# A transformer layer on eight cores: first projection started behind a quarter of the input, value projection in half-size groups with two store queues

## What is computed

```python
q, k, v = (proj(wq), proj(wk), proj(wv))          # x @ w.T, split in 16 heads
q, k = apply_rope(q, k, sin, cos)
att = softmax(einsum('bhqd,bhkd->bhqk', q, k) / sqrt(HD))
y = einsum('bhqk,bhkd->bhqd', att, v)             # then y @ wo.T
x = layernorm(x + attention)
x = layernorm(x + ffn(x))                         # gate, up, silu, down; int weights
```

## Time and profile before

| | us |
|---|---|
| median of 3 runs | 4934.71 |
| lowest of them | 4930.45 |
| the profiled execution | 4929.0 |
| its span on the slowest core (core 1) | 4927.5 |
| spans of the eight cores | 4909.2 to 4927.5 |

### The profile page before, as it was taken

The page is one execution under the profiler, slowest core; times in us unless marked ns, Lnnn a source line. Parts: engine busy times, 40 slices in busy tenths (PEclk is TensorE's granted clock), DMA queues, the critical chain, the costliest instruction groups (busy, mean ns, idle before and its releaser), DMA issues.

```text
span 4927.5 us, 42276 instructions; the slowest of 8 cores (4909.2 to 4927.5 us)
## 1 busy us (share of the span) xinstructions
PE 3875.9 (79%) x15680; PEld 1494.9 (30%) x15680; DVE 635.9 (13%) x1592; ACT 1313.9 (27%) x1073; POOL 357.5 (7%) x680
## 2 busy tenths in 40 slices
PE   3999766677777777777967999989921999998870
PEld 1444322211111111112423444433310444443330
DVE  0222000001010000101220000011121000011122
ACT  0111101343434333343442333300022333320003
POOL 0000000000000000000000000012200000002220
PEclk9999888888878787888988999998965999999995
DMA  6334310110100101001574444344435444434443
GB/s 121 58 75 96 70 40 26 29 22 14 26 13 13 26 13 26 13 13 26 167 192 81 75 76 77 71 65 60 61 86 120 77 76 75 75 68 63 63 53 119
DMA packets 200713, 310.96 MB, mean 63 GB/s; under 512 B 99265, under 2 KB 152642, under 8 KB 191682
## 3 DMA queue, kind: packets, MB, share of 16 engines
q0 software_dynamic: 97344, 188.85, 23.9%
q1 hardware_dynamic: 103170, 119.41, 8.1%
HBM read 412.86 MB, written 58.72 MB: 96 GB/s over the span
## 4 chain that ended last, share of the span: by engine, by line
PE 66%; DMA 16%; ACT 5%; DVE 5%; issue 5%; another core or an unknown queue 2%; SPq 0%; DVEq 0%; ACTq 0%; POOLq 0%; POOL 0%
PE PS L585 12%; PE PS L592 12%; PE PS L478 9%; DMA AB<-wd_c 7%; PE PS L530 6%; PE PS L526 5%; PE PS L493 5%; PE PS L563 5%; PE PS L606 4%; PE PS L515 4%; ACT AB L639 3%; PE PS L518 3%; DMA AB<-AB 2%; DMA v_sp<-AB 2%; DMA AB<-x1b 2%
## 5 line engine op out<-in xcount | busy, mean ns | idle before, releaser
L585 PE MATMUL PS<-AB 128*128 128x512 bf16 x2816 | 627.1, 381 | 267.9 <-DMA AB<-x1b 267.9
L639 ACT ACTIVATE AB<-PS,AB 128x1024 bf16<-128x1024 f32 x512 | 563.1, 1113 | 853.0 <-PE PS L518 853.0
L606 PE MATMUL PS<-AB 128*128 128x512 bf16 x2816 | 672.3, 397 | 83.4 <-DVE AB L794 82.1
L592 PE MATMUL PS<-AB 128*128 128x512 bf16 x2816 | 622.1, 379 | 0.0
L478 PE MATMUL PS<-AB 128*128 128x512 bf16 x2048 | 445.1, 381 | 78.1 <-DMA AB<-wq_c 78.1
L515 PE MATMUL PS<-AB 128*128 128x512 bf16 x512 | 247.3, 483 | 299.4 <-DVE AB L744 277.6
L585 PEld LDWEIGHTS PS<-AB 128*128 128x128 bf16 x2816 | 276.8, 98 | 604.1 <-issue 275.3
L526 PE MATMUL PS<-AB 128*128 128x512 bf16 x896 | 393.7, 439 | 37.1 <-ACT AB L639 37.1
L606 PEld LDWEIGHTS PS<-AB 128*128 128x128 bf16 x2816 | 273.7, 101 | 482.0 <-issue 265.8
L530 PE MATMUL PS<-AB 128*1 128x512 bf16 x896 | 377.4, 421 | 0.0
L592 PEld LDWEIGHTS PS<-AB 128*128 128x128 bf16 x2816 | 275.3, 98 | 332.5
(11 more groups left out here) (71 smaller groups left out, 1741.9 us busy)
## 6 DMA issues: line engine op xcount, KB each, us to landing
AB<-wg_c POOLq DMA_DIRECT2D x88, 512.0 KB, 6.1
AB<-wu_c POOLq DMA_DIRECT2D x88, 512.0 KB, 8.1
AB<-wd_c POOLq DMA_DIRECT2D x352, 128.0 KB, 2.9
AB<-x SPq DMA_DIRECT2D x16, 1024.0 KB, 6.6
x1f<-AB SPq DMA_DIRECT2D x16, 1024.0 KB, 4.9
AB<-x1f SPq DMA_DIRECT2D x16, 1024.0 KB, 6.7
out<-AB SPq DMA_DIRECT2D x16, 1024.0 KB, 4.7
AB<-xT POOLq DMA_DIRECT2D x16, 512.0 KB, 33.3
```

The lines of the kernel that those rows point to most:

```text
L585: mm = t.matmul(bank(par * 4 + cch)[:, 0:512], GDQ[par][:, di * 128:(di + 1) * 128], X1T[:, di * 1024 + cch * 512: di * 1024 + (cch + 1) * ...
L592: mm = t.matmul(bank(par * 4 + 2 + cch)[:, 0:512], UDQ[par][:, di * 128:(di + 1) * 128], X1T[:, di * 1024 + cch * 512: di * 1024 + (cch + ...
L606: mm = t.matmul(bank(tt)[:, 0:512], HT[:, h2 * 1024 + tt * 128: h2 * 1024 + (tt + 1) * 128], WDQ[i % 2][:, 0:512], start=(h2 == 0), stop=( ...
L639: sc.activation(PT[u % 4], bank(2 * (u % 2), 2)[:, 0:1024], AF.Exp, bias=CVC[:, 0:1], scale=ASCL).then_inc(s2sc, 1)
```

## The change

It has two parts. At the start, POOL issues only four blocks of the input, then the first two query weights, then the other twelve blocks in three batches of four, each batch after everything of the batches before has landed, and the value weight last. PE waits for a quarter of the input at a time during its first head block. In the value projection there are 16 groups of 64 matmuls that alternate between the two halves of PSUM, so that PE waits only for the copies of the group before the last; the staging buffer has four parts; the even stores stay on SP's queue, and the odd ones are issued by ACT itself on its own queue (semaphore `s1spv`). The rest of the program is as before; two scratch areas move to make room.

```diff
-    VST = [bf16(OFF_VSTG + i * 1024, 128, 512) for i in range(2)]
+    VST = [bf16(OFF_VSTG + i * 1024, 128, 512) for i in range(4)]
...
 sync
-            for i in range(64):
-                jb, tt = divmod(i, 8)
-                dc, th = divmod(jb, 2)
+            for i2 in range(32):
+                i = 2 * i2
+                j2, t2 = divmod(i, 4)
+                dc, q = divmod(j2, 4)
                 s.wait_ge(s1scb, i + 1)
-                if i >= 1:
-                    s.wait_ge(s1spb, 16 * i)
-                s.dma_start(out=v_sp[th * 8 + tt][:, dc * 512:(dc + 1) * 512],
-                            in_=VST[i % 2]).then_inc(s1spb, 16)
+                if i2 >= 1:
+                    s.wait_ge(s1spb, 16 * i2)
+                s.dma_start(out=v_sp[q * 4 + t2][:, dc * 512:(dc + 1) * 512],
+                            in_=VST[i % 4]).then_inc(s1spb, 16)
...
 gpsimd
-            for dt in range(NDI):
+            for dt in range(4):
                 g.dma_start(out=XT[:, dt * 2048:(dt + 1) * 2048],
                             in_=xT_h[dt * 128:(dt + 1) * 128, :]).then_inc(s0x, 16)
+            if PH >= 1:
+                g.dma_start(out=WB[0], in_=wq_h[0]).then_inc(s1w[0], 16)
+                g.dma_start(out=WB[1], in_=wq_h[1]).then_inc(s1w[1], 16)
+            for b in range(1, 4):
+                g.wait_ge(s0x, 16 * 4 * b)
+                for dt in range(4 * b, 4 * b + 4):
+                    g.dma_start(out=XT[:, dt * 2048:(dt + 1) * 2048],
+                                in_=xT_h[dt * 128:(dt + 1) * 128, :]).then_inc(s0x, 16)
...
-                    g.wait_ge(s1pb, 2 * (dc - 1))
+                    g.wait_ge(s1pb, 4 * (dc - 1))
...
 tensor
-            t.wait_ge(s0x, 16 * NDI)
...
                 for di in range(NDI):
+                    if j == 0 and di % 4 == 0:
+                        t.wait_ge(s0x, 16 * min(4 * (di // 4 + 1), NDI))
...
-            for jb in range(8):
-                dc, th = divmod(jb, 2)
-                if th == 0:
+            for j2 in range(16):
+                dc, q = divmod(j2, 4)
+                if q == 0:
                     t.wait_ge(s1vw[dc % 2], 16 * (dc // 2 + 1))
-                if jb >= 1:
-                    t.wait_ge(s1scb, jb * 8)
+                if j2 >= 2:
+                    t.wait_ge(s1scb, 4 * (j2 - 1))
                 for di in range(NDI):
-                    for tt in range(8):
-                        tg = th * 8 + tt
-                        mm = t.matmul(bank(tt)[:, 0:512],
+                    for t2 in range(4):
+                        tg = q * 4 + t2
+                        mm = t.matmul(bank((j2 % 2) * 4 + t2)[:, 0:512],
...
 scalar
+            def vspill(i):
+                j2s, t2s = divmod(i, 4)
+                dcs, qs = divmod(j2s, 4)
+                sc.wait_ge(s1scb, i + 1)
+                if i >= 3:
+                    sc.wait_ge(s1spv, 16 * ((i - 1) // 2))
+                sc.dma_start(out=v_sp[qs * 4 + t2s][:, dcs * 512:(dcs + 1) * 512],
+                             in_=VST[i % 4]).then_inc(s1spv, 16)
+            for j2 in range(16):
+                sc.wait_ge(s1pb, j2 + 1)
+                for t2 in range(4):
+                    i = j2 * 4 + t2
+                    if i >= 4:
+                        sc.wait_ge(s1spb if i % 2 == 0 else s1spv,
+                                   16 * ((i - 4) // 2 + 1))
+                    sc.copy(VST[i % 4], bank((j2 % 2) * 4 + t2)[:, 0:512]).then_inc(s1scb, 1)
+                    if i >= 2 and i % 2 == 0:
+                        vspill(i - 1)
+            vspill(63)
```

More of the change, by code:

```diff
@@ L41 @@
 OFF_SDB   = 203888
-OFF_SPC   = 199168
-OFF_SPC2  = 200192
+OFF_SPC   = 200704
+OFF_SPC2  = 201728
 OFF_XT    = 0
@@ L230, in build_program @@
     s1v1 = sem("s1v1"); s1sw = sem("s1sw"); s1v2 = sem("s1v2"); s1sp = sem("s1sp")
-    s1vw = [sem("s1vwA"), sem("s1vwB")]; s1pb = sem("s1pb"); s1scb = sem("s1scb"); s1spb = sem("s1spb")
+    s1vw = [sem("s1vwA"), sem("s1vwB")]; s1pb = sem("s1pb"); s1scb = sem("s1scb"); s1spb = sem("s1spb"); s1spv = sem("s1spv")
     s2kv = [sem("s2kvA"), sem("s2kvB")]; s2st = sem("s2st"); s2pv = sem("s2pv"); s2sc = sem("s2sc")
@@ L288, in _ @@
                 s.wait_ge(s1sp, 16 * 16)
-                s.wait_ge(s1spb, 16 * 64)
+                s.wait_ge(s1spb, 16 * 32)
+                s.wait_ge(s1spv, 16 * 32)
                 if DEBUG:
@@ L397, in _ @@
             g.dma_start(out=VW[0], in_=wv_h[0]).then_inc(s1vw[0], 16)
-            for j in range(32):
+            for j in range(2, 32):
                 src = wq_h[j] if j < 16 else wk_h[j - 16]
-                if j >= 2:
-                    g.wait_ge(s1pe, j - 1)
-                    g.wait_ge(s1w[j % 2], 16 * (j // 2))
+                g.wait_ge(s1pe, j - 1)
+                g.wait_ge(s1w[j % 2], 16 * (j // 2))
                 g.dma_start(out=WB[j % 2], in_=src).then_inc(s1w[j % 2], 16)
```

## The result

The changed kernel takes 4777.95 us (median of 10 runs) against 4934.79 us for the kernel before (median of 10). Their ratio is 0.9687, with a 95% interval of 0.9675 to 0.9698. The forecast was 4788 us with a range of 4763 to 4814: it held, and the size was right within 10 us of 157. That it came so near is partly luck. One of its terms, the stall at a reload, was wrong by 14.7 us, and another one, the start, by 4 us in the opposite direction.

A forecast was written before the change was run, and what follows sets the result against it. PE's two waits, 78.1 us before the first matmul and 118.5 us in the value projection, were taken to bound the kernel. Gains 15.6 + 127.9 = 143.5 us off 4929.0 gave 4785.5, plus 3: 4788 us, range 4763 to 4814.

The forecast's parts named there:

- Part 1, the start: Start, up to the end of head block 1: it ends at 93.3 us instead of 108.9, gain 15.6 us.
- the dry queue: Start: behind input batches 2 and 3 nothing is queued, costing 2.4 us for each of two batches.
- the lower bound: Start: the last input block lands at 68.0 us if the load queue never runs dry.
- Part 2, PE's work: Value projection: PE's matmuls take 16 x 13.81 = 221.0 us, with all seven 12.4 us gaps gone.
- Part 2, the stalls: Value projection, third and fourth weight reloads: PE stalls 5.35 us at each, 10.7 us, plus 4.0 us for the clock.
- Part 2, the end: End of value projection: three chained stores on ACT, 7.0 us until SP may load k and v, before 15.6.
- Rival 1: Value projection: stores pass the reload over two queues, no stall; gain 158.2 us, time 4774 us; chance 0.20.
- Rival 2: Start gains only 0 to 8.6 us, queue dry longer or block 2's weight late; 4795 to 4804 us; chance 0.12.
- Rival 3: Value projection: granted clock does not hold high without rests; 5009 us worst, 4839 at 13/16 clock; chance 0.04.
- the prediction's sign: PE's matmuls: the forecast is wrong if the granted clock leaves 1.00 while PE is busy; no size given.
- Rival 4: Value projection: ACT's and SP's stores disturb each other, 16.9 us a store; time 5102 us; chance 0.02.
- Rival 5: Value projection: PE still waits for the current group's copies, so the change does not do what it says; chance 0.02.

## Why the prediction was right, and where it was wrong

**What bounds the kernel.** Right. The two waits lay on the chain, and what was taken from them came off the end; the rest of the program is as long as before within a few microseconds.

**Part 1, the start.** Forecast 15.6 us, measured 11.7 on average over the cores. The mis-sized term is the dry queue: 2.4 us for each of two batches. On core 2 PE's bursts start at 42.48, 59.42 and 77.11, so the third batch took 16.9 us and the fourth 17.7, where 13.8 + 2.4 = 16.2 was forecast, and the second ended at 42.4 instead of 40.4. Without the waits the bursts are 12.3 and 12.2 us apart (43.54, 55.80, 67.96 on core 3), the whole comes to the 68.0 of the lower bound, and the two batches cost 8.1 instead of 4.8. The slow matmuls after the idle time cost 1.7 us instead of 3.2, and the copy of block 1 came at 96.15 against 93.3. PE's first matmul was forecast near 25 us; it came at 33.6, although the first four blocks had landed by 21.69, when POOL issued the next ones. The row names the input; by the row of the run without batch waits it was held by small tables that I had not looked at, but that time is hidden by the later quarters. The weight of block 2 was in time, as forecast: PE ran on through 192 matmuls.

**Part 2, PE's work.** 221.0 forecast; measured 222.9 on five cores and 221.2 on the three others. The difference is a short stretch at the low clock just after the 2.3 us wait ahead of the stage, while PE is busy. Core 2:

```profile
513.80:517.00 3.20, 3.20 (x9) 1.10 (x8) 1.19 (x2) 0.00 (x0) 0.00 (x0) 0.50 0.23 52
517.20:735.60 218.40, 218.40 (x1012) 98.82 (x1010) 1.22 (x1) 33.32 (x60) 1.58 (x3) 1.00 0.28 68
```

The prediction had put nothing for it. In the kernel before it came on five cores too, but not on core 1, from which the forecast was made.

**Part 2, the stalls.** This is the step that failed: "Store 11 is issued about 0.7 us after the group's end, behind the reload by 0.2 us". It was issued 0.33 us ahead of it. I had let a DMA issue on ACT wait for the end of the copy that stands before it in the list, where it waits only for its semaphore; and the whole term hung on 0.2 us. With the store held back by one copy, the stall appeared, 5.1 to 10.3 us per core for both reloads instead of the 10.7 forecast, since the reloads landed sooner (13.8 to 17.4 us) than what I took from core 1.

**Part 2, the end.** 7.0 forecast, 743.02 - 735.63 = 7.4 measured on core 2 and 6.9 on average, 1.6 us less than with one queue by the run without the second (8.5).

**The sum.** On core 2 the value projection took 230.3 us against 242.8, so 12.5 too much was forecast here, and 2.9 too little at the start (93.3 against 96.15). The load of k was forecast at 752.7 and came 9.6 us earlier. From there on this core took 3.1 us longer than core 1 before, which leaves 6.5 us in the profiled execution. The rest is the step to the median: I had added 3 us, rounded down by half a microsecond, and the median lies 1.1 us below the profiled execution. So a forecast that had only left out the stall (14.7 us) would have said 4773 and been 5 us low: the errors offset each other in part.

**The rivals.** Rival 1 came nearer to the time (4774) than the forecast did, but not by its mechanism: stores do not pass a reload. In the changed kernel store 13 and SP's store 12, both behind it, took 15.9 and 17.1 us, and the store held back by one copy took 13.6 to 17.5. Here the trace again disagrees with what the page "DMA: Bandwidth & Descriptors" of the Trainium skill says in "Queues, rings and completion order" on turns between queues, now for a second queue as well. Rival 2 was half right in size (4 us lost at the start) for its first reason, the dry queue. Rival 3 falls for this stage: past the short stretch shown above the granted clock stayed at 1.00 over the rest of the 223 us of matmuls without a gap, and its mean over the whole was 0.99 to 1.00 on all eight cores of the profiled execution. By the letter of the prediction's sign (the clock leaves 1.00 while PE is busy) that stretch counts against it, at a price of 1.7 us. The level of 13/16 does occur in this case, for 154 us in the last stage of the kernel before, but on two cores of a die and not on the two others. Rival 4 falls: on core 2 half of ACT's stores take 1.8 us or less. Rival 5 falls with PE's table of waits.

## What to carry to other kernels

When an engine waits for its accumulators to be copied out, alternate between two halves of PSUM first: here that alone gave 127 of 141 us, and once the halves alternated, more staging buffers only mattered where a store got stuck behind a large load, and a second store queue hardly at all. Where a small transfer and a large one are issued close together, find out which goes first to a tenth of a microsecond and from the wait of the issue itself, not from the instruction in front of it; better, give the small one slack enough to lose. Issue independent loads at once with a semaphore for each part that is waited for, rather than in batches that wait for each other.

## What was not expected of the hardware

A 128 KB store issued 0.05 us ahead of a 2 MB load (625.66 and 625.71) landed by 629.33 at the latest, 2.1 to 3.6 us after its issue over the eight cores, and one issued 0.25 us behind such a load landed 14 to 18 us later, within half a microsecond of the load itself, from either queue. What in the DMA engines makes it so, no run here shows. And a DMA in ACT's list is issued while the copy ahead of it is still running (570.13 within the copy from 570.00 to 570.58). The granted clock fell to 0.50 for a moment after a wait of 2.3 us in front of the value projection on five of eight cores, and not on the three others. What decides between them, no run here shows.
